# Another order for the first four units of a clustering-and-convolution kernel, with identity products ahead of them

## The chip, the cores and the metric

One core of a Trainium2 chip runs the kernel. The metric is device time in microseconds for one launch, the median of three runs; lower is better.

## The reference

The input `x` is 8 images of 512 channels and 32 x 48 = 1536 pixels, in float32. There are 40 centroids of 512 channels, a 512 x 512 weight matrix and a bias.

```python
xn = x / norm(x, axis=1); cn = centroids / norm(centroids, axis=1)
sim = einsum('bchw,nc->bnhw', xn, cn)
idx = argmax(sim, axis=1)
onehot = one_hot(idx, N)
sum_x = einsum('bhwn,bchw->bnc', onehot, x)
centroids_local = sum_x / maximum(sum(onehot, axis=(1, 2)), 1.0)[..., None]
gathered = centroids_local[arange(B)[:, None, None], idx]
delta = transpose(gathered, (0, 3, 1, 2)) - x
alpha = exp(-mean(delta * delta, axis=1, keepdims=True))
y = x + alpha * delta
out = relu(einsum('oc,bchw->bohw', W, y) + b)
```

So each pixel finds its nearest centroid by cosine, each image makes its own means of the pixels of a cluster, each pixel is pulled towards its cluster's mean, and a 1 x 1 convolution with bias and relu follows.

## The kernel before

The work is cut into 24 units of 512 pixels, three to an image; unit g belongs to image g // 3. Channels lie on partitions in four blocks of 128. Each engine has a list of instructions of its own, written out by hand in the order in which it runs them, and semaphores tie the lists together. Nothing is reordered: an instruction that waits holds back all behind it on its engine.

Image b's first half is the clustering. `similarities(g)` on TensorE makes products of 64 x 256 with the centroids as weights (L696). `copy_sims` on ScalarE keeps the result (L546). `transpose_sims` brings the similarities of the image into pixels by centroids (L705). `argmax` is five VectorE operations (L320 to L332) that give `oh`, the one-hot. `copy_onehot` makes bfloat16 copies of it (ScalarE, L551), `transpose_onehot` transposes it (TensorE, L720), `evacuate_onehot` copies it out and counts it (ScalarE, L558), and `counts` on VectorE turns the counts into reciprocals (L338, L340). `sum_clusters(b, u)` (TensorE, L737) sums the pixels of a cluster; for that it needs x with pixels on partitions, in `XT`. ScalarE keeps the high half of the sums (`copy_sums`, L564), VectorE the rest (`low_clusters`, L345), TensorE adds the two column halves (`add_halves`, L748 and L749), ScalarE scales them (`means`, L569 and L572), and VectorE splits them into three bfloat16 parts (L351, L354) and writes them to `G` (L359).

Its second half goes unit by unit: `gather(g, h)` (TensorE, L768) multiplies G by the one-hot; `delta` (VectorE, L366) subtracts x; `square` (ScalarE, L513) and `add_squares` (VectorE, L372 to L376), `high_sum` (L518), `low_sum` (L381) and `sum_squares` (TensorE, L775 and L776; L782 for units 0 and 1, in float32) give the mean square; `exp` (L522), `scale` (L386) and `y_half` (GpSimd L281, for unit 0 VectorE L394) give y; `high_half` (ScalarE, L527) and `low_half` (GpSimd, L288) split y into two parts; `convolve` (L794 to L796) makes three products for each pair of blocks, and `relu` (L535) writes the output tile. The convolution runs two units behind the gather.

How `XT` is filled differs. For image 0 TensorE transposes x in blocks (`transpose_x(u, half)`, L806: half 0 into `main`, half 1 into `gat`), and VectorE (`keep_transposed(u)`, L303, half 0 of units 0 and 1) or ScalarE (L502, the others) copies the result out of PSUM. From image 1 on x is loaded a second time in blocks of 32 channels (`load_xs`, L210, four transfers of 256 KB per unit), and VectorE transposes these in 32 x 32 squares (`transpose_half(g, h)`, L311); the second one signals `tr_done`, on which `load_xs(g + 4)` and later waits.

The loads are all issued on SyncE's queue, in the order of its list: centroids, x of units 0 to 2, the weights, the bias, x of units 3 and 4, the blocks of unit 3, x of unit 5, the blocks of unit 4, and so on. x loads are L204. The weights `W` are transposed on TensorE (`transpose_weights`, L820) once the copies of x have left `main` and `gat`.

The order on TensorE at the start is written at L830 to L849: similarities 0, both halves of unit 0's transposes, similarities 1 and 2, and so on. ScalarE's stands at L590 to L630.

```python
            similarities(0)
            transpose_x(0, 0)
            transpose_x(0, 1)
            similarities(1)
            similarities(2)
            transpose_x(1, 0)
            transpose_sims(0)
            transpose_x(1, 1)
```

Of the kernel before, what the change touches and what calls it, by code (L numbers as in the profile page):

```python
# [14 lines left out]
P = 128  # L15
# [3 lines left out]
PARTS = HW // UNIT  # L19
# [43 lines left out]
def build(nc, x, cent, w, bias, out):  # L63
# [3 lines left out]
    with ctx:  # L67
# [130 lines left out]
        def _(sp):  # L198
# [24 lines left out]
            with nc.allow_non_contiguous_dma(reason="512 bias values, once"):  # L223
                sp.dma_start(bcol[:, :], bias.rearrange("(k p) -> p k", p=P)).then_inc(b_in, 16)
            load_x(3)
            load_x(4)
            load_xs(3)
            load_x(5)
# [69 lines left out]
        def _(dve):  # L298
            v_ = nc.vector

            def keep_transposed(u):
                dve.wait_ge(xp_done, 2 * u + 1)
                v_.tensor_copy(XT[:, u, 0:HALF, :], main[:, :, :]).then_inc(xe_dve, 1)  # L303

# [121 lines left out]
            dve.wait_ge(const_done, 7)  # L426
            keep_transposed(0)
            keep_transposed(1)
            argmax(0)
            for k in range(KC):  # L430
                low_weights(k)
            low_clusters(0)
            counts(0)
            transpose_half(3, 0)
            rest_of_mean(0)
            parts_of_mean(0)

            transpose_half(3, 1)
            for g in range(DIRECT):
# [57 lines left out]
        def _(act):  # L497
# [91 lines left out]

            copy_sims(0)  # L590
            keep_transposed(0, 1)
            copy_sims(1)
            copy_sims(2)
            keep_transposed(1, 1)
            keep_transposed(2, 0)
# [24 lines left out]
            relu(0, 1)  # L620
            high_half(1, 1)
            square(2, 0)
            copy_sums(1)
            square(2, 1)
            evacuate_onehot(1)
            means(1)
            high_sum(2)
            relu(0, 2)
# [48 lines left out]
        def _(pe):  # L677
# [45 lines left out]
            def sum_clusters(b, u):  # L723
                if u == 0:
                    pe.wait_ge(oh_done, b + 1)
                    wait(pe, sumsL_done, b)
                if b > 0:
                    pe.wait_ge(tr_done, PARTS * (b - 1) + u + 1)
                elif u < PARTS - 1:
                    pe.wait_ge(xe_dve, u + 1)  # L730
                    pe.wait_ge(xe_act, u + 1)
                else:
                    pe.wait_ge(xe_act, PARTS + 1)
                for t in range(HALF):
                    for h in range(2):
                        tile = HALF * h + t
                        last = t_.matmul(sumP[NPAD * h:NPAD * (h + 1), :], oh[:, slot(u, tile), :],  # L737
                                         XT[:, u, tile, :], start=(u == 0 and t == 0),
                                         stop=(u == PARTS - 1 and t == HALF - 1))
                last.then_inc(c_done, 1)  # L740
# [60 lines left out]
            def transpose_x(u, half):  # L801
                wait(pe, (xe_dve, xe_act)[half], u)
                for t in range(HALF):
# [4 lines left out]
                last.then_inc(xp_done, 1)  # L808

            pe.wait_ge(ident_done, 5)  # L810
            pe.wait_ge(c_in[0], 16)
            for k in range(KC):
                last = t_.transpose(sumP[:, k * N:(k + 1) * N], craw[0:N, k * P:(k + 1) * P], ident[0:N, 0:N])
            last.then_inc(cT_ps, 1)
            pe.wait_ge(cT_done, 2)
            def transpose_weights(k):
                pe.wait_ge(w_in, 16)
                pe.wait_ge(xe_act, 3 if k < 2 else 4)
                for o in range(KC):
# [10 lines left out]
            similarities(0)  # L830
            transpose_x(0, 0)
            transpose_x(0, 1)
            similarities(1)
            similarities(2)
# [99 lines left out]
```

## Time and profile before

| what | value |
|---|---|
| median of 3 runs | 435.92 us (435.83 to 436.05) |
| the profiled execution's own time | 435.22 us |
| its span, first to last instruction | 433.4 us |
| TensorE busy | 420.2 us (97%), 2112 instructions |
| VectorE busy | 286.6 us (66%) |
| ScalarE busy | 242.4 us (56%) |
| GpSimd busy | 206.5 us (48%) |
| chain that ended last | TensorE 92%, GpSimd 2%, ScalarE 2% |
| DMA | 73.94 MB, mean 171 GB/s |

The span is what the profile's rows cover; 1.8 us of the profiled time lie around it. The chain is followed back from the last instruction, at each step to what released it. A busy share is an average over the span; the stages at the start differ from the rest, and for them the timeline is read. In the rows, PE is TensorE, DVE VectorE, ACT ScalarE, POOL GpSimd and SP SyncE. A float32 product stands in the timeline as two passes, a 128 x 128 transpose as one.

### The profile page before, as it was taken

What the parts mean: (1) busy time and instruction counts of PE and PEld (TensorE: products, weight loads), DVE (VectorE), ACT (ScalarE), POOL (GpSimd) and SP (SyncE); (2) the same over time, 40 slices, a digit from 0 to 9 for tenths busy, and PEclk for the clock granted to TensorE, in tenths of its full rate; (3) what the DMA queues carried; (4) which work ended last, traced back from release to release, by engine and by line L of the source; (5) the groups of instructions that cost most, each with busy time, mean ns of one, the idle gap of its engine ahead of it and who ended that gap; (6) DMA issues with size and microseconds to landing.
All of it is one profiled execution on the core that took longest, in us unless ns stands there. A gap on an engine that the chain in (4) does not pass through costs nothing.

```text
span 433.4 us, 5744 instructions
## 1 busy us (share of the span) xinstructions
PE 420.2 (97%) x2112; PEld 292.9 (68%) x2112; DVE 286.6 (66%) x378; ACT 242.4 (56%) x328; POOL 206.5 (48%) x102
## 2 busy tenths in 40 slices
PE   4999989999999999999999999999999999999997
PEld 2745446775777767775767757776677758777785
DVE  2549959495684767586773956857674956777730
ACT  5465374565563674554754665646735647555542
POOL 2000572585373681764644852835816645334330
PEclk9999999999999999999999999999999999999999
DMA  8996296977489755859279664888564220222133
GB/s 285 343 228 131 49 255 174 280 226 181 133 210 241 190 198 112 240 143 284 97 195 228 196 161 147 228 208 200 189 140 151 99 97 2 98 98 97 42 113 136
DMA packets 70927, 73.94 MB, mean 171 GB/s; under 512 B 2724, under 2 KB 45732, under 8 KB 70900
## 3 DMA queue, kind: packets, MB, share of 16 engines
q1 hardware_dynamic: 70900, 73.58, 61.4%
q8 instruction: 17, 0.28, 0.3%
q14 instruction: 10, 0.08, 0.1%
HBM read 48.40 MB, written 25.17 MB: 170 GB/s over the span
## 4 chain that ended last, share of the span: by engine, by line
PE 92%; POOL 2%; ACT 2%; DMA 1%; DVE 1%; issue 1%; SPq 0%
PE main L794 20%; PE main L796 20%; PE main L795 20%; PE fa L696 10%; PE sump L737 9%; PE gat L768 5%; PE al L775 1%; DMA x<-x 1%; POOL yl L288 1%; PE fa L705 1%; PE al L776 1%; PE fa L720 1%; POOL z L281 1%; PE gat L782 1%; PE al L782 1%; ACT oht L558 1%
## 5 line engine op out<-in xcount | busy, mean ns | idle before, releaser
L281 POOL TENSOR_TENSOR z<-z,x 128x1024 f32<-128x1024 f32 x42 | 99.3, 2383 | 154.3 <-DVE z L386 154.3
L794 PE MATMUL main<-yh,wh 128*128 128x512 f32 x376 | 153.1, 407 | 0.0
L796 PE MATMUL main<-yh,wl 128*128 128x512 f32 x376 | 147.2, 391 | 0.0
L795 PE MATMUL main<-yl,wh 128*128 128x512 f32 x376 | 147.0, 391 | 0.0
L288 POOL TENSOR_TENSOR yl<-z,yh 128x1024 fp32r<-128x1024 f32 x44 | 105.8, 2420 | 54.9 <-ACT yh L527 54.9
L366 DVE TENSOR_TENSOR z<-gat,x 128x1024 f32<-128x1024 f32 x46 | 56.1, 1220 | 91.4 <-PE gat L768 91.3
L535 ACT ACTIVATE o<-main,bcol 128x512 f32<-128x512 f32 x96 | 65.8, 687 | 85.4 <-PE main L796 85.4
L794 PEld LDWEIGHTS main<-yh,wh 128*128 128x128 f32 x376 | 70.6, 188 | 20.8 <-issue 4.6
L796 PEld LDWEIGHTS main<-yh,wl 128*128 128x128 f32 x376 | 70.6, 188 | 15.8
L795 PEld LDWEIGHTS main<-yl,wh 128*128 128x128 f32 x376 | 70.8, 188 | 14.5
L527 ACT ACTIVATE yh<-z 128x1024 fp32r<-128x1024 f32 x48 | 50.5, 1052 | 22.9 <-POOL z L281 21.9
L386 DVE TENSOR_TENSOR z<-z,al 128x1024 f32<-128x1024 f32 x46 | 53.9, 1211 | 1.5 <-ACT al L522 1.5
L311 DVE STREAM_TRANSPOSE xt<-xs 128x1024 f32<-128x1024 f32 x42 | 51.0, 1228 | 0.0
L696 PE MATMUL fa<-x,c_t 128*64 128x256 f32 x384 | 46.7, 394 | 3.5 <-DMA x<-x 3.2
L737 PE MATMUL sump<-xt,oh 128*64 128x512 f32 x192 | 43.6, 598 | 0.0
L696 PEld LDWEIGHTS fa<-x,c_t 128*64 128x64 f32 x384 | 27.4, 140 | 21.4 <-issue 10.7
L513 ACT ACTIVATE sq<-z 128x1024 f32<-128x1024 f32 x22 | 23.3, 1060 | 21.9 <-DVE z L366 21.9
L513 ACT ACTIVATE gat<-z 128x1024 f32<-128x1024 f32 x22 | 22.6, 1027 | 18.8 <-DVE z L366 18.8
L737 PEld LDWEIGHTS sump<-xt,oh 128*64 128x64 f32 x192 | 12.9, 136 | 25.5 <-issue 25.5
L768 PE MATMUL gat<-oht,g 120*128 120x512 bf16 x92 | 27.9, 385 | 0.4 <-DVE g L359 0.2
L518 ACT ACTIVATE sh<-al 128x512 fp32r<-128x512 f32 x22 | 13.2, 598 | 8.7 <-DVE al L376 8.7
L522 ACT ACTIVATE al<-al 128x512 f32<-128x512 f32 x23 | 13.6, 590 | 7.8 <-PE al L776 6.5
(111 smaller groups left out, 316.6 us busy)
## 6 DMA issues: line engine op xcount, KB each, us to landing
x<-x SPq DMA_DIRECT2D x24, 1024.0 KB, 5.5
out<-o SPq DMA_DIRECT2D x23, 1024.0 KB, 4.7
xs<-x SPq DMA_DIRECT2D x84, 256.0 KB, 5.8
o<-w SPq DMA_DIRECT2D x1, 1024.0 KB, 11.9
out<-o SPq DMA_DIRECT2D x4, 256.0 KB, 2.1
sq<-centroids SPq DMA_DIRECT2D x2, 80.0 KB
bcol<-bias SPq DMA_DIRECT2D x1, 2.0 KB, 11.5
```

Source lines behind the costliest of these rows:

```text
L281: pool.tensor_tensor(z, z, X[g // PARTS % 2][:, pair(h), span(g)], ALU.add).then_inc(y_pool, 1)
L288: pool.tensor_tensor(YL[g % 2][:, pair(h), :], Z[g % 2][:, pair(h), :], YH[g % 2][:, pair(h), :].bitcast(F32), ALU.subtract).then_inc(lo_p ...
L311: last = v_.transpose(XT[:, g % PARTS, :, :].rearrange("p t (m j) -> p m t j", j=BLK)[:, blocks, :, :], XS[g % 2][:, blocks, :])
L366: v_.tensor_tensor(Z[g % 2][:, pair(h), :], banks(g, h)[:, :, :], X[g // PARTS % 2][:, pair(h), span(g)], ALU.subtract).then_inc(z_done, 1)
L386: v_.tensor_tensor(z, z, alpha(g).unsqueeze(1).to_broadcast([P, 2, UNIT]), ALU.mult).then_inc(za_done, 1)
L527: a_.activation(YH[g % 2][:, pair(h), :], Z[g % 2][:, pair(h), :], ACT.Copy).then_inc(hi_done, 1)
L535: a_.activation(OUT[g % 2][:, o, :], main[:, o % 2, :], ACT.Relu, bias=bcol[:, o:o + 1]).then_inc(relu_done, 1)
L696: last = t_.matmul(simP[u][NPAD * h:NPAD * (h + 1), :], cT[:, k, :], toks, start=(k == 0), stop=(k == KC - 1))
L737: last = t_.matmul(sumP[NPAD * h:NPAD * (h + 1), :], oh[:, slot(u, tile), :], XT[:, u, tile, :], start=(u == 0 and t == 0), stop=(u == PAR ...
L794: t_.matmul(main[:, o % 2, :], WH[:, k, rows], YH[g % 2][:, k, :], start=(k == 0), stop=False)
L795: t_.matmul(main[:, o % 2, :], WH[:, k, rows], YL[g % 2][:, k, :], start=False, stop=False)
L796: last = t_.matmul(main[:, o % 2, :], WL[:, k, rows], YH[g % 2][:, k, :], start=False, stop=(k == KC - 1))
```

## The change

Five things are done, all in the first four units.

- TensorE multiplies the identity by itself into `al`, twice ahead of the centroids' transposes and nine times behind them (`keep_busy`). The result is not used.
- TensorE's order: similarities 1 now stands ahead of the second half of unit 0's transposes, so similarities 2 comes behind it. ScalarE's copies follow this.
- Half 0 of unit 1's transposed x is copied out by ScalarE and no longer by VectorE; the waits on `xe_dve` and `xe_act` are renumbered.
- VectorE's two transposes of unit 3's blocks stand ahead of the low half of the cluster sums and ahead of the counts; before, one stood behind the counts and one behind G. SyncE issues the blocks of unit 3 ahead of x of unit 4.
- ScalarE, in image 1: the one-hot's evacuation stands ahead of the upper squares of unit 2, and the upper high half of unit 1 behind the means.

```diff
             load_x(3)
+            load_xs(3)
             load_x(4)
-            load_xs(3)
             load_x(5)
...
-            keep_transposed(0)
-            keep_transposed(1)
+            keep_transposed()
             argmax(0)
             for k in range(KC):
                 low_weights(k)
+            transpose_half(3, 0)
             low_clusters(0)
+            transpose_half(3, 1)
             counts(0)
-            transpose_half(3, 0)
             rest_of_mean(0)
             parts_of_mean(0)
 
-            transpose_half(3, 1)
...
             copy_sims(0)
+            copy_sims(1)
             keep_transposed(0, 1)
-            copy_sims(1)
             copy_sims(2)
+            keep_transposed(1, 0)
             keep_transposed(1, 1)
...
-            high_half(1, 1)
             square(2, 0)
             copy_sums(1)
+            evacuate_onehot(1)
             square(2, 1)
-            evacuate_onehot(1)
             means(1)
+            high_half(1, 1)
             high_sum(2)
...
+            def keep_busy(times):
+
+                for _ in range(times):
+                    t_.matmul(al[:, 0:P], ident[:, :], ident[:, :], start=True, stop=True)
+
             pe.wait_ge(ident_done, 5)
+            keep_busy(2)
             pe.wait_ge(c_in[0], 16)
...
             last.then_inc(cT_ps, 1)
+            keep_busy(9)
             pe.wait_ge(cT_done, 2)
...
             similarities(0)
             transpose_x(0, 0)
+            similarities(1)
             transpose_x(0, 1)
-            similarities(1)
             similarities(2)
```

TensorE from its first instruction to the first weights' transposes, before (`sump` holds the centroids' transposes, `fa` the similarities, `main` and `gat` the transposed x):

```order
L813 MATMUL sump<-ident,sq 128x40 x4
L696 MATMUL fa<-x,c_t 64x256 x8
L806 MATMUL main<-ident,x 128x128 x8
L806 MATMUL gat<-ident,x 128x128 x8
L696 MATMUL fa<-x,c_t 64x256 x16
L806 MATMUL main<-ident,x 128x128 x8
L705 MATMUL fa<-ident,sims 128x128 x6
L806 MATMUL gat<-ident,x 128x128 x8
L806 MATMUL main<-ident,x 128x128 x8
L806 MATMUL gat<-ident,x 128x128 x8
L820 MATMUL main<-ident,o 128x128 x8
```

and with the change, whose line numbers differ by a few:

```order
L815 MATMUL al<-ident 128x128 x2
L821 MATMUL sump<-ident,sq 128x40 x4
L815 MATMUL al<-ident 128x128 x9
L696 MATMUL fa<-x,c_t 64x256 x8
L808 MATMUL main<-ident,x 128x128 x8
L696 MATMUL fa<-x,c_t 64x256 x8
L808 MATMUL gat<-ident,x 128x128 x8
L696 MATMUL fa<-x,c_t 64x256 x8
L808 MATMUL main<-ident,x 128x128 x8
L705 MATMUL fa<-ident,sims 128x128 x6
L808 MATMUL gat<-ident,x 128x128 x8
L808 MATMUL main<-ident,x 128x128 x8
```

The identity products stand around the centroids' transposes, and the first 24 similarities and 16 transposes alternate in groups of eight; from the transposes of unit 1 on the order is the old one.

VectorE behind the low halves of the weights, to unit 0's first delta (L311 transposes unit 3's blocks, L345 is the low half of the sums, L338 and L340 are the counts, L351 to L359 make G), one piece of the difference:

```order
-L345 TENSOR_TENSOR sums_l<-sump,sums_h 128x512
-L338 TENSOR_SCALAR cols<-cols 120x1
-L340 RECIPROCAL cols<-cols 120x1
-L311 STREAM_TRANSPOSE xt<-xs 128x8x4x32
+L311 STREAM_TRANSPOSE xt<-xs 128x8x4x32
+L345 TENSOR_TENSOR sums_l<-sump,sums_h 128x512
+L311 STREAM_TRANSPOSE xt<-xs 128x8x4x32
+L338 TENSOR_SCALAR cols<-cols 120x1
+L340 RECIPROCAL cols<-cols 120x1
 L351 SCALAR_TENSOR_TENSOR al<-part,cols,al 120x512
 L354 CAST part<-al 120x512
 L359 SCALAR_TENSOR_TENSOR g<-part,cols,al 120x512
-L311 STREAM_TRANSPOSE xt<-xs 128x8x4x32
 L366 TENSOR_TENSOR z<-gat,x 128x1024
```

Both transposes moved: the first from behind the counts to ahead of the low half, the second from behind G to ahead of the counts.

ScalarE in image 1, from the first relu of unit 0 to the means (L513 squares, L564 the sums, L558 the one-hot's evacuation, L569 and L572 the means, L527 a high half), before:

```order
L535 ACTIVATE o<-main,bcol 128x512 x2
L527 ACTIVATE yh<-z 128x1024
L513 ACTIVATE sq<-z 128x1024
L564 ACTIVATE sums_h<-sump 128x512
L513 ACTIVATE gat<-z 128x1024
L558 ACTIVATE oht,cols<-fa 120x1536
L569 ACTIVATE fa<-fa,cols 120x512
L572 ACTIVATE part<-fa 120x512
L518 ACTIVATE sh<-al 128x512
```

and with the change:

```order
L534 ACTIVATE o<-main,bcol 128x512 x2
L512 ACTIVATE sq<-z 128x1024
L563 ACTIVATE sums_h<-sump 128x512
L557 ACTIVATE oht,cols<-fa 120x1536
L512 ACTIVATE gat<-z 128x1024
L568 ACTIVATE fa<-fa,cols 120x512
L571 ACTIVATE part<-fa 120x512
L526 ACTIVATE yh<-z 128x1024
L517 ACTIVATE sh<-al 128x512
```

The upper high half of unit 1 moved from the second row to the last but one, and the evacuation moved past one square.

## Rows read from the trace of the kernel before

**Rows 1.** Windows, all engines: stretch, length, busy us (count), clock, DMA, GB/s.
```profile
100.00:200.00 100.00, 100.00 (x507) 70.31 (x506) 69.27 (x82) 57.69 (x78) 56.76 (x24) 1.00 0.69 188
```

**Rows 2.** Timeline, PE, 0 to 35 us: start, us, engine, line, what [idle before].
```profile
2.84 0.62 PE L813 MATMUL sump<-ident,sq 40*128 40x40 f32 x4 [2.84 <-DMA sq<-centroids]
...
6.68 3.68 PE L696 MATMUL fa<-x,c_t 128*64 128x256 f32 x16 [3.23 <-DMA x<-x]
...
12.26 3.67 PE L696 MATMUL fa<-x,c_t 128*64 128x256 f32 x32
...
21.66 1.94 PE L737 MATMUL sump<-xt,oh 128*64 128x512 f32 x8
...
34.65 0.60 PE L768 MATMUL gat<-oht,g 120*128 120x512 bf16 x2 [0.24 <-DVE g L359]
```

**Rows 3.** Timeline: PE's float32 products of 512 columns, GpSimd's identity.
```profile
39.23 3.60 PE L782 MATMUL al<-o,ones 128*128 128x512 f32 x8
...
42.66 3.60 PE L782 MATMUL gat<-o,ones 128*128 128x512 f32 x8
...
1.52 0.29 POOL L261 TENSOR_SCALAR_AFFINE_SELECT ident<-ident 128x128 f32<-128x128 f32 x1 [0.24 <-POOL cols L259]
```

**Rows 4.** SP issues at 2.1, 18.0, 19.4, landings, all x loads' landings, one window.
```profile
2.13 0.93 SPq L204 DMA_DIRECT2D x<-x  x2
...
DMA to landing us min/median/max: 7.4/8.5/9.6
...
18.02 1.30 SPq L210 DMA_DIRECT2D xs<-x  x1
...
xs<-x SPq DMA_DIRECT2D x1, 256.0 KB, 10.1
...
19.36 3.12 SPq L204 DMA_DIRECT2D x<-x  x1
...
DMA to landing us min/median/max: 5.3/9.6/14.6
...
17.00:18.00 1.00, 1.00 (x12) 1.00 (x11) 1.00 (x1) 0.00 (x0) 0.00 (x0) 1.00 1.05 397
```

**Rows 5.** Timeline, DVE and ACT, 18 to 36 us.
```profile
18.13 0.65 DVE L320 TENSOR_REDUCE best<-fa 128x12 f32<-128x480 f32 x1
...
29.05 1.45 ACT L558 ACTIVATE oht<-fa 120x1536 bf16<-120x1536 bf16 x1 [0.20 <-PE fa L720]
...
30.62 0.15 DVE L338 TENSOR_SCALAR cols<-cols 120x1 f32<-120x1 f32 x1 [1.05 <-ACT oht L558]
...
30.89 1.25 DVE L311 STREAM_TRANSPOSE xt<-xs 128x1024 f32<-128x1024 f32 x1
...
33.85 0.75 DVE L359 SCALAR_TENSOR_TENSOR g<-part,cols,al 120x512 bf16<-120x512 bf16 x1
...
35.67 1.19 DVE L366 TENSOR_TENSOR z<-gat,x 128x1024 f32<-128x1024 f32 x1
```

**Rows 6.** Timeline, ACT, PE, DVE and POOL, 57 to 69 us.
```profile
57.96 1.06 ACT L527 ACTIVATE yh<-z 128x1024 fp32r<-128x1024 f32 x1
...
60.35 1.02 ACT L513 ACTIVATE gat<-z 128x1024 f32<-128x1024 f32 x1
...
61.30 1.44 ACT L558 ACTIVATE oht<-fa 120x1536 bf16<-120x1536 bf16 x1
...
62.88 0.49 PE L748 MATMUL fa<-sums_h,select 128*120 128x512 f32 x1 [1.99 <-ACT oht L558]
...
63.12 0.67 DVE L372 TENSOR_TENSOR sq<-sq,gat 128x512 f32<-128x512 f32 x1
...
67.31 0.74 DVE L359 SCALAR_TENSOR_TENSOR g<-part,cols,fa 120x512 bf16<-120x512 bf16 x1
...
68.36 0.59 PE L794 MATMUL main<-yh,wh 128*128 128x512 f32 x1
...
57.89 4.69 POOL L288 TENSOR_TENSOR yl<-z,yh 128x1024 fp32r<-128x1024 f32 x2
```

More of the change, by code:

```diff
@@ L299, in _, with keep_transposed @@
             v_ = nc.vector
-            def keep_transposed(u):
-                dve.wait_ge(xp_done, 2 * u + 1)
-                v_.tensor_copy(XT[:, u, 0:HALF, :], main[:, :, :]).then_inc(xe_dve, 1)
+            def keep_transposed():
+                dve.wait_ge(xp_done, 1)
+                v_.tensor_copy(XT[:, 0, 0:HALF, :], main[:, :, :]).then_inc(xe_dve, 1)
             def transpose_half(g, h):
@@ L728, in sum_clusters @@
                     pe.wait_ge(tr_done, PARTS * (b - 1) + u + 1)
-                elif u < PARTS - 1:
-                    pe.wait_ge(xe_dve, u + 1)
-                    pe.wait_ge(xe_act, u + 1)
-                else:
-                    pe.wait_ge(xe_act, PARTS + 1)
+                else:
+                    pe.wait_ge(xe_dve, 1)
+                    pe.wait_ge(xe_act, 2 * u + 1)
                 for t in range(HALF):
@@ L801, in transpose_x @@
             def transpose_x(u, half):
-                wait(pe, (xe_dve, xe_act)[half], u)
+                if (u, half) == (1, 0):
+                    pe.wait_ge(xe_dve, 1)
+                elif u > 0:
+                    pe.wait_ge(xe_act, 2 * (u - 1) + half)
                 for t in range(HALF):
@@ L817, in transpose_weights @@
                 pe.wait_ge(w_in, 16)
-                pe.wait_ge(xe_act, 3 if k < 2 else 4)
+                pe.wait_ge(xe_act, 4 if k < 2 else 5)
                 for o in range(KC):
```

## The prediction

> **What bounds the kernel now.** I read three views in order. First the windows: from 100 to 200 us TensorE is busy for all of the 100 us [rows 1], and the shares of the page say the same of the whole (97%). So the steady part is a fixed amount of TensorE work, and a change to the first 70 us can only move it as a block, by the idle or slow TensorE time that it removes there. Second, TensorE's own timeline, to find such time [rows 2]. There are three stretches. (a) The first similarities take 3.68 us for 16 passes, from 6.68; the next row has 32 of the same passes in 3.67 us. TensorE had done 0.62 us of work, at 2.84, and was idle until x landed. The granted clock column shows 1.00 in all windows, but the durations show the lower level (1.2 GHz) in the first and the higher (2.4 GHz) in the second; everything after 10.30 runs at the higher. (b) From 29.05 [rows 5] to 34.65 [rows 2] the mean of image 0 is made on ScalarE and VectorE, with little TensorE work beside it. (c) Before 62.88 TensorE is idle for 1.99 us, waiting for ScalarE's one-hot evacuation [rows 6]. Third, what ends these: the loads [rows 4], the mean chain [rows 5] and ScalarE's order in image 1 [rows 6].
>
> **Step 1, products with the identity.** 2 + 9 products, 128 columns each, in float32. The trace has none. The nearest row is the 512-column float32 product: 8 passes, four products, start to start 3.43 us (39.23 to 42.66), so 0.86 us each and by columns 0.215 us for 128 at the high level, 0.43 at the low one [rows 3]. The identity is ready at 1.52 + 0.29 = 1.81 [rows 3], so two products run 1.9 to 2.8, just before the centroid transposes at 2.84, which end at 3.46; a delay of 0.1 us there is covered, because the similarities wait for x until 6.68 [rows 2]. The other nine take 3.9 us at the low level and end at 7.3; if the level rises as long after the start of work as it did in this trace (6.68 to 10.30, 3.6 us, so at about 5.5), five of them are slow, four are fast, and they end near 6.5. I estimate an overrun over 6.68 of 0.2 us (bounds 0 and 0.6). The first similarities then take 1.84 instead of 3.68: a gain of 1.84 less 0.2. Bounds: 1.84, and, if nothing rises in time, a loss of 0.6.
>
> **Step 2, unit 2's similarities earlier, copies moved.** The same TensorE work as before stands from there to 21.66, in another order, so only new waits count. Similarities 0 end at 8.5 to 8.7, the eight transposes at 9.6 (0.97 us: sixteen of them stand between 10.30 and 12.26). Unit 1's x was issued at 2.13 and takes 7.4 us: 9.5, and the start about 0.13 later, as at 6.68; unit 2's takes 9.6 from about 2.6: 12.2 [rows 4]. The walk then reads: similarities 1 until 11.5, transposes 12.5, similarities 2 until 14.3, half 0 of unit 1's transposes 15.2, the transposed similarities 15.9. So there are waits of 0.1 to 0.2 us for x, in total 0.2. VectorE loses one copy to ScalarE and starts the argmax at 16.0 instead of 18.13; its five operations, of 0.65 us like the first [rows 5], take 3.4 us with their gaps, so the one-hot is there at 19.4. ScalarE now has four copies of 1.03 us in a row, from 15.3 to 20.2, each released by a block of transposes of the same length; as before, TensorE waits some 0.2 us for one of them, a wait that exists already. The cluster sums of unit 0 start at 20.1 instead of 21.66 [rows 2]. What remains of step 1 and 2: 1.84 - 0.2 - 0.2, **1.4 us**.
>
> **Step 3, VectorE's transposes and the load order.** Each of unit 3's two transposes takes 1.25 us. They stood in the mean chain: one at 30.89, beside ScalarE's means, and one behind G, which kept delta at 35.67 although G was done at 33.85 + 0.75 = 34.60 [rows 5]. Now the first stands ahead of the low half of the cluster sums, the second between it and the counts. The chain's times shift by 1.4: ScalarE keeps the sums at 26.9 and gives the one-hot at 30.60 - 1.4 = 29.2 (evacuation 29.05 plus 1.45 and the count [rows 5]). The first transpose fits if unit 3's blocks have landed by 26.1; the second runs 28.1 to 29.3 beside the evacuation, so the counts start 0.1 late at most. The blocks: the last was issued at 18.02 and took 10.1 us, 28.1 [rows 4]. The change puts them ahead of unit 4's x, 1.05 MB at 397 GB/s, so 2.6 us earlier [rows 4]: 25.5. It fits by 0.6 us. Unit 4's x falls back to where the blocks were, 28.1 at most; its similarities come at 31.1. Unit 5's, issued at 19.36, lands by 34.0 even with the longest time seen, 14.6 [rows 4], and its similarities start at 34.2. Delta gains 0.4 us more than TensorE, but TensorE has similarities 5 in between and did not wait for delta, so I cost that at nothing. The first gather moves from 34.65 to 33.25: the 1.4 us are kept. From there to 58 us everything is the old order, shifted; GpSimd's chain begins with unit 0's high half, which shifts too.
>
> **Step 4, ScalarE in image 1.** Before: high half (1,1) at 57.96, square (2,0), sums, square (2,1) at 60.35, evacuation 61.30 to 62.83, TensorE on at 62.88 [rows 6]. Now (in the times of before) square (2,0) starts at 57.8, the sums at 58.7, the evacuation when TensorE's one-hot transposes end, 59.45, and it is done at 61.0. TensorE reaches the sum of halves at 60.9: its wait of 1.99 goes to 0.1, **1.85 us gained** there. What is late next: square (2,1) runs 60.9 to 61.9 (before it ended at 61.37), and VectorE's in-order row behind it starts at 61.95 instead of 63.12: squares, rest of the mean, low sum, G, in all 4.93 us (63.12 to 67.31 + 0.74 [rows 6]), so G is there at about 66.7 against 68.05. TensorE, 1.85 early, would reach unit 3's gather at 66.3 and waits 0.4 for it. What remains is **1.4 us** (bounds: 0, if the chain behind square (2,1) does not move, and 1.85). High half (1,1) goes from 57.96 to about 63.4 to 64.4, behind the means; GpSimd then needs 2.35 us for its low half (4.69 for two), 66.8. TensorE wants it in the middle of the convolution that started at 68.36, seven products in, now at 68.5: covered, by 1.7 us [rows 6].
>
> **The sum.** 1.4 + 1.4 = 2.8 us. The profiled execution took 435.22, so it would be 432.4; the median of the runs shown, 435.92, is 0.7 above it, and against that I forecast **433.1**. A measurement can tell about 0.2%, 0.9 us, from no change.
>
> **Rivals.** *The clock does not rise in time* (chance 0.15). The products may be too few, or too loosely spaced around 2.8 us, so that the similarities start at 7.3 and still take 3.68: steps 1 and 2 lose 0.6 instead of gaining 1.4, the whole gains 0.8, 435.1. For it: the only rise in the trace came after 3.6 us of dense work. Against it: the products offer 4.8 us of nearly dense work before x lands. The Trainium skill (TensorE: Matmul & The Clock Gate, Part 1) says that the point of the rise differs from run to run of the same kernel. By that the executions would scatter by up to 1.8 us of lost or gained clock; the three runs lie within 0.22 us of each other, so the runs here speak against it, and that is why this rival gets no more.
>
> *Only step 1 to 3 pays* (0.12). ScalarE's new order moves the wait from 62.88 to unit 3's gather, with the sum of squares and G later than worked out: the whole gains 1.4, 434.5. For it: G was done at 68.05, and the convolution behind unit 3's gather started at 68.36, so G already bounds together with TensorE.
>
> *Unit 3's blocks land late* (0.10, of it 0.04 slower). VectorE is in order, and the first transpose now stands ahead of the sums' low half, the counts, the mean and G. The point from which it costs is a landing at 26.1; after that each us late is a us. At 28.1, the old landing, the counts start at 28.1 + 1.25 + 0.65 + 1.25 = 31.25 instead of 30.62: steps 1 to 3 lose 0.6, the whole gains 0.8, 435.1. From 28.9 on the kernel is **slower**: with the last block issued at 18.02 and the longest time of any x load, 14.6, it would be 32.6, 3.7 us over the old time, 439.6; in the middle, at 30.7, 437.7. Against it: the same bytes with one megabyte less ahead.
>
> **How the numbers follow.** The forecast has 0.60 and its own bounds (overrun 0 to 0.6, G's 0 to 0.4) give 432.3 to 433.8; the three rivals 0.37; 0.03 is left for more than I count. The range 432.2 to 435.0 takes the forecast, the second rival and the cases between it and the first. Faster by over 0.2%: 0.60 + 0.12 + 0.03 and most of the cases between forecast and first and third rival, 0.87; within 0.2%: 0.09; slower: 0.04.
>
> **What would show it.** Right: the similarities of unit 0 have 16 passes in about 1.8 us and start at 6.7 to 6.9; the one-hot is done by 19.5; unit 3's first transpose starts by 26.1 with no wait behind it; the first gather is at about 33.2; the wait before the sum of halves of image 1 is under 0.3 us and unit 3's gather comes 2.8 us earlier, at 65.3. Wrong: passes of 630 ns at 6.7 us, VectorE idle before the first transpose beyond 26.1, or a new TensorE wait at the low half (1,1).

## The result and the profile after

| | before | with the change |
|---|---|---|
| median of 6 runs each | 435.99 us (435.75 to 436.52) | 433.12 us (432.35 to 433.72) |
| ratio, 95% interval | | 0.9931 [0.9918, 0.9944] |
| the profiled execution | 435.22 us, span 433.4 | 433.72 us, span 431.9 |
| TensorE busy | 420.2 us (97%) | 424.5 us (98%) |
| TensorE's share of the chain | 92% | 95% |

The ratios here and below are of the means. One execution of the kernel before, among those run beside e5 to e8, took 533.62 us at a mean granted clock of 0.757 and is in no comparison.

The median fell by 2.87 us where 2.8 were forecast. But the two profiled executions are only 1.5 us apart, so a profile read against a profile shows half of the gain, and the first question is where the other half is. The table already gives part of the answer: the profiled execution of before is faster than all six timed ones, and that of the change is the slowest of its six.

The window of the steady part is what it was [rows 1]:

```profile
100.00:200.00 100.00, 100.00 (x508) 70.39 (x506) 68.59 (x83) 57.92 (x78) 56.79 (x24) 1.00 0.70 188
```

TensorE's timeline of the change answers to [rows 2] (start, us, engine, line, what):

```profile
1.87 1.23 PE L815 MATMUL al<-ident 128*128 128x128 f32 x4 [1.87 <-POOL ident L261]
3.03 0.65 PE L821 MATMUL sump<-ident,sq 40*128 40x40 f32 x4
3.61 4.21 PE L815 MATMUL al<-ident 128*128 128x128 f32 x18
7.74 2.43 PE L696 MATMUL fa<-x,c_t 128*64 128x256 f32 x16
10.11 1.09 PE L808 MATMUL main<-ident,x 128*128 128x128 f32 x8
...
21.64 1.94 PE L736 MATMUL sump<-xt,oh 128*64 128x512 f32 x8
...
34.64 0.60 PE L767 MATMUL gat<-oht,g 120*128 120x512 bf16 x2 [0.24 <-DVE g L359]
```

The two first products take 1.16 us up to the centroids' transposes, which are 0.2 late, and the nine take 4.13 us, 0.46 each: all at the lower level (421 ns is the median of a pass, against 274 to 275 ns in the faster part of e6 below). The similarities begin at 7.74, 1.06 later than in the trace of before, and are themselves slow for a while: 2.37 us up to 10.11, where 1.88 is the time at the higher level. The clock rose at about 8.8 (if t us were slow, t/3.62 + (2.37 - t)/1.88 = 1, so t = 1.0), not at 5.5. The cluster sums start at 21.64 against 21.66: in this execution steps 1 and 2 of the prediction gave nothing.

VectorE, 17 to 36 us, against [rows 5]:

```profile
17.69 0.66 DVE L320 TENSOR_REDUCE best<-fa 128x12 f32<-128x480 f32 x1 [5.16 <-PE fa L705]
...
26.04 1.23 DVE L311 STREAM_TRANSPOSE xt<-xs 128x1024 f32<-128x1024 f32 x1
...
29.47 1.23 DVE L311 STREAM_TRANSPOSE xt<-xs 128x1024 f32<-128x1024 f32 x1
30.63 0.13 DVE L338 TENSOR_SCALAR cols<-cols 120x1 f32<-120x1 f32 x1
...
33.83 0.75 DVE L359 SCALAR_TENSOR_TENSOR g<-part,cols,al 120x512 bf16<-120x512 bf16 x1
35.28 1.23 DVE L366 TENSOR_TENSOR z<-gat,x 128x1024 f32<-128x1024 f32 x1 [0.70 <-PE gat L767]
```

The first transpose starts as soon as VectorE is free, with no wait for its blocks. The second ends just as the counts can start. Delta now starts 0.39 us earlier than it did.

Image 1, against [rows 6], in the order PE, ACT, DVE, POOL:

```profile
45.98 1.94 PE L736 MATMUL sump<-xt,oh 128*64 128x512 f32 x8
60.95 0.49 PE L747 MATMUL fa<-sums_h,select 128*120 128x512 f32 x1 [0.18 <-ACT oht L557]
65.99 0.47 PE L774 MATMUL al<-sh,ones 128*128 128x512 f32 x1 [0.22 <-DVE sl L381]
66.56 0.60 PE L767 MATMUL gat<-oht,g 120*128 120x512 bf16 x2
66.81 0.59 PE L793 MATMUL main<-yh,wh 128*128 128x512 f32 x1
...
59.35 1.45 ACT L557 ACTIVATE oht<-fa 120x1536 bf16<-120x1536 bf16 x1
60.79 1.02 ACT L512 ACTIVATE gat<-z 128x1024 f32<-128x1024 f32 x1
63.25 1.05 ACT L526 ACTIVATE yh<-z 128x1024 fp32r<-128x1024 f32 x1
...
61.84 0.69 DVE L372 TENSOR_TENSOR sq<-sq,gat 128x512 f32<-128x512 f32 x1 [0.57 <-ACT gat L512]
65.77 0.73 DVE L359 SCALAR_TENSOR_TENSOR g<-part,cols,fa 120x512 bf16<-120x512 bf16 x1
...
64.38 2.39 POOL L288 TENSOR_TENSOR yl<-z,yh 128x1024 fp32r<-128x1024 f32 x1 [4.13 <-ACT yh L526]
```

This is step 4 as it was read: TensorE's wait of 1.99 is 0.18, the new bound is the low sum and G behind the upper squares (a wait of 0.22 at 65.99), and GpSimd's low half, 64.38 to 66.8, ends before it is wanted. From the first cluster sums of image 1 to unit 3's gather it was 68.11 - 46.19 = 21.92 us and is 66.56 - 45.98 = 20.58: 1.34 gained, forecast 1.4.

Four of the signs that the prediction named for being right fail in this execution: the similarities of unit 0 start at 7.74 and not by 6.9, the argmax starts only at 17.69 (its five operations end at 21.1, not by 19.5), the first gather is at 34.64 and not near 33.2, and unit 3's gather at 66.56 and not at 65.3. A better execution comes close (e4, below: similarities at 6.91, gathers at 33.32 and 65.22).

### The profile page after: what moved, and what is told of

Read it like the earlier page. It is cut to its first block, busy times and chain, and to the rows that moved or that the text cites. A ratio compares the mean times of both kernels' runs of the same rounds, so it can differ in the third digit from the quotient of the medians.

```text
span 431.9 us, 5788 instructions
## 1 busy us (share of the span) xinstructions
PE 424.5 (98%) x2134; PEld 296.9 (69%) x2134; DVE 285.3 (66%) x377; ACT 243.7 (56%) x329; POOL 206.8 (48%) x102
## 4 chain that ended last, share of the span: by engine, by line
PE 95%; DVE 2%; ACT 1%; issue 1%; POOL 0%; POOLq 0%; DVEq 0%
PE main L793 20%; PE main L795 19%; PE main L794 19%; PE sump L736 10%; PE fa L696 9%; PE gat L767 5%; PE al L774 1%; PE al L815 1%; PE fa L705 1%; PE al L775 1%; PE fa L720 1%; PE main L836 1%; PE al L781 1%; PE gat L781 1%; DVE xt L311 1%; PE gat L808 1%
## 5 line engine op out<-in xcount | busy, mean ns | idle before, releaser
L311 DVE STREAM_TRANSPOSE xt<-xs 128x1024 f32<-128x1024 f32 x42 | 51.0, 1228 | 0.0
L696 PE MATMUL fa<-x,c_t 128*64 128x256 f32 x384 | 45.7, 386 | 0.3 <-ACT oht L557 0.3
L736 PEld LDWEIGHTS sump<-xt,oh 128*64 128x64 f32 x192 | 12.8, 136 | 25.5 <-issue 25.5
## 6 DMA issues: line engine op xcount, KB each, us to landing
o<-w SPq DMA_DIRECT2D x1, 1024.0 KB, 12.2
bcol<-bias SPq DMA_DIRECT2D x1, 2.0 KB, 11.7
```

What stands on the lines that cost most here:

```text
L311: last = v_.transpose(XT[:, g % PARTS, :, :].rearrange("p t (m j) -> p m t j", j=BLK)[:, blocks, :, :], XS[g % 2][:, blocks, :])
L696: last = t_.matmul(simP[u][NPAD * h:NPAD * (h + 1), :], cT[:, k, :], toks, start=(k == 0), stop=(k == KC - 1))
```

## Experiments

The runs came in three sets, e1 to e4, e5 to e8 and e9 to e12, each on a chip of its own, with the kernel before run beside each set. Its median was 435.91, 435.85 and 435.56 us, so between sets a difference of 0.3 us says little. My theory after reading both traces: ScalarE's order gives its 1.4 to 1.5 us in every execution, and the products give the rest through the clock, by an amount that differs from execution to execution. Rivals: the new order of similarities, copies and loads gives the rest; or the products cost what they give.

### The parts alone

`e1_no_products`, the change without its products:

```diff
-            keep_busy(2)
...
-            keep_busy(9)
```

> The change without its eleven identity products. Theory (the clock is worth 1.3 us in the median, ScalarE's order in image 1 the rest, 1.55): 434.4 against 436.0 before, and in the profile the first similarities start at 6.7 and need about 3.6 us. Rival (the new order of similarities, copies and loads brings the 1.3 us, the products nothing): 433.1. Rival 2 (the products cost as much as they give): 433.1 or less as well.

`e2_products_only`, before with the products:

```diff
+            keep_busy(2)
             pe.wait_ge(c_in[0], 16)
...
+            keep_busy(9)
             pe.wait_ge(cT_done, 2)
```

> The kernel before with the eleven products and nothing else. Theory: 434.7, with a larger scatter between the executions than the kernel before, because the point at which the clock rises moves from run to run; the first similarities start between 6.7 and 7.8 and take 1.8 to 3.7 us. Rival (order): 436.0.

`e3_act_order_only`, before with ScalarE's order:

```diff
-            high_half(1, 1)
             square(2, 0)
             copy_sums(1)
+            evacuate_onehot(1)
             square(2, 1)
-            evacuate_onehot(1)
             means(1)
+            high_half(1, 1)
```

> The kernel before with only ScalarE's new order in image 1. Theory: 1.55 us less than before, 434.4; TensorE's wait before the sum of halves of image 1 falls from 1.99 to under 0.3 us and unit 3's first convolution starts 1.5 us earlier. Rival (the wait only moves to unit 3's gather): 435.5 or more.

`e4_seven`, the change with seven products in place of nine:

```diff
-            keep_busy(9)
+            keep_busy(7)
```

> The change with 7 instead of 9 products behind the centroids' transposes. Theory (nine overrun x's landing by up to 1.0 us when all of them run at the low level, 4.21 us for nine): 432.8, up to 0.5 us less than the change where the clock rises late, the same where it rises early. Rival (the last two products are what brings the rise ahead of the similarities): 433.5 or more.

| run | median us (lowest to highest), executions | ratio to before [95%] |
|---|---|---|
| e1, no products | 433.81 (433.61 to 434.19), 5 | 0.9955 [0.9942, 0.9968] |
| e2, products only | 434.63 (433.85 to 436.22), 12 | 0.9978 [0.9965, 0.9991] |
| e3, ScalarE's order only | 434.07 (433.89 to 434.72), 5 | 0.9964 [0.9952, 0.9975] |
| e4, seven products | 433.15 (432.40 to 433.33), 5 | 0.9936 [0.9924, 0.9949] |

The kernel before stood at 435.91 there (435.02 to 436.49, 17 executions). ScalarE's order alone takes 1.84 off the median, the products alone 1.28, and without the products the change loses 0.7. So the rival that gave the rest to the new orders falls with e1, though by less than forecast (433.81, not 434.4). The parts add up to more than the whole (1.84 + 1.28 against 2.87): with five executions in a run, a median carries some tenths of a us of scatter. In the trace of e3 the wait before the sum of halves is 0.18:

```profile
61.94 0.49 PE L748 MATMUL fa<-sums_h,select 128*120 128x512 f32 x1 [0.18 <-ACT oht L558]
```

Both e3 and e1 have the first similarities at the lower level throughout; e1's rows:

```profile
6.66 3.68 PE L696 MATMUL fa<-x,c_t 128*64 128x256 f32 x16 [3.09 <-DMA x<-x]
10.27 1.22 PE L808 MATMUL main<-ident,x 128*128 128x128 f32 x8
```

With seven products the median is that of nine; the expected 432.8 was not reached. Its profiled execution (432.40) shows what a good one looks like: similarities at the high level from their first pass, waiting for x where in the change x waited for them, and the cluster sums at 20.32.

```profile
3.60 3.15 PE L815 MATMUL al<-ident 128*128 128x128 f32 x14
6.91 1.95 PE L696 MATMUL fa<-x,c_t 128*64 128x256 f32 x16 [0.16 <-DMA x<-x]
...
20.32 1.94 PE L736 MATMUL sump<-xt,oh 128*64 128x512 f32 x8
```

What was not expected stands in e2. Its 12 executions are two groups: seven from 433.85 to 435.00 with a mean granted clock of 1.000, and five from 435.61 to 436.22 with 0.996. The profiled one (435.61) is of the second group. Its windows (stretch, length, busy PE, PEld, DVE, ACT, POOL, clock, DMA, GB/s) and its PE rows in image 1:

```profile
60.00:62.00 2.00, 0.01 (x1) 0.01 (x1) 0.32 (x2) 1.94 (x3) 1.70 (x1) 0.99 1.22 206
62.00:63.00 1.00, 1.00 (x3) 0.79 (x3) 0.96 (x4) 0.00 (x0) 0.00 (x0) 0.50 1.22 217
...
65.00:66.00 1.00, 1.00 (x5) 0.77 (x5) 0.97 (x2) 0.69 (x2) 0.00 (x0) 0.81 1.04 383
```

```profile
61.99 0.78 PE L748 MATMUL fa<-sums_h,select 128*120 128x512 f32 x1 [2.01 <-ACT oht L558]
62.57 0.63 PE L749 MATMUL fa<-sums_l,select 128*120 128x512 f32 x1
...
65.72 0.40 PE L795 MATMUL main<-yl,wh 128*128 128x512 f32 x1
```

The granted clock falls to 0.50, the lower level, at the end of the 2.01 us in which TensorE waits for ScalarE's evacuation, and comes back at about 65.4 (0.81 is the mean of the window from 65 to 66). Meanwhile products start 0.43 us apart instead of 0.23, and 1.5 us are lost: from the first cluster sums of image 1 to the gather it is 68.73 - 45.28 = 23.45 us instead of 21.92. Half the clock for 3.4 us takes 0.4% off the mean over the span, which is what a mean of 0.996 says. The kernel before has the same wait, 1.99 us in its profiled execution, and a mean clock of 1.000 in all 17 executions.

### Undoing one step each, and moving the products

`e5_old_act`, the change with ScalarE's order put back (the diff of e3, reversed).

> The change with ScalarE's order in image 1 put back to the old one. Theory (with the products the clock falls to the lower level in some executions, when TensorE idles 2.0 us before the sum of halves of image 1, as in the run with the products alone): two groups of executions, one near 434.0 with a granted clock of 1.000 and one 1.7 us above it with 0.996; median between 434.0 and 435.7. Rival (that fall belonged to the old order of similarities or loads): one group near 434.7, clock 1.000 in all.

`e6_products_act`, before with the diffs of e2 and e3 and nothing else.

> The kernel before with the products and ScalarE's new order in image 1, without the new orders of similarities, copies, transposes and loads. Theory (those orders bring 0.3 us or less): 433.0 to 433.4, granted clock 1.000 in every execution. Rival (the new orders are worth 1 us, since x's similarities follow its landing): 434.0 or more.

`e7_old_loads`, the change with the old order of loads:

```diff
             load_x(3)
-            load_xs(3)
             load_x(4)
+            load_xs(3)
```

> The change, but unit 3's blocks are issued behind unit 4's x, as before. Theory (VectorE runs in order, and a landing later than 26.1 holds back the counts and G): the first transpose starts at about 28.1, the counts at about 31.2, the first gather at 35.2 or 35.3 whatever the clock did, so 434.4, with a smaller scatter than the change. Rival (the transposes' place makes no difference): 433.1.

`e8_early`, the change with the products on a tile of their own:

```diff
+            v_.memset(hot[:, :], 1.0).then_inc(hot_done, 1)
             v_.memset(cT[:, :, N:NPAD], 0.0).then_inc(cT_done, 1)
...
-                    t_.matmul(al[:, 0:P], ident[:, :], ident[:, :], start=True, stop=True)
+                    t_.matmul(al[:, 0:P], hot[:, :], hot[:, :], start=True, stop=True)
...
+            pe.wait_ge(hot_done, 1)
+            keep_busy(4)
             pe.wait_ge(ident_done, 5)
-            keep_busy(2)
...
-            keep_busy(9)
+            keep_busy(7)
```

> The change with the products on a tile that VectorE fills as its first operation: four ahead of the centroids' transposes, from 1.0 us instead of 1.87, and seven behind them. Theory (the earlier dense work starts, the earlier the clock rises in the unlucky executions): 432.8, and the slowest execution 433.3 or less. Rival (the point of the rise does not follow the start of the work that closely): 433.1, scatter as in the run with seven.

| run | median us (lowest to highest), executions | ratio to before [95%] |
|---|---|---|
| e5, change with ScalarE's old order | 434.26 (433.71 to 436.40), 12 | 0.9980 [0.9965, 0.9995] |
| e6, products and ScalarE's order | 432.90 (432.30 to 433.10), 5 | 0.9928 [0.9916, 0.9940] |
| e7, change with the old loads | 435.61 (433.85 to 438.20), 12 | 1.0002 [0.9981, 1.0023] |
| e8, products early | 432.58 (432.29 to 432.65), 5 | 0.9923 [0.9911, 0.9935] |

The kernel before stood at 435.85 there (434.90 to 436.53, 22 executions).

e5 falls into the two groups that the theory named: seven executions from 433.71 to 434.30 with a clock of 1.000, five from 435.94 to 436.40 with 0.996. Its profiled execution is of the first group: TensorE waits 2.11 us before the sum of halves and the clock does not fall. So such a wait does not bring the fall each time, and where the clock fell in the other five is not shown.

e6 is as fast as the change (a little below the 433.0 to 433.4 expected), so steps 2 and 3, the orders of similarities, copies, transposes and loads, bring nothing together that these runs can tell. The intervals of the timelines say why. From the transposes behind the first similarities to the cluster sums it is 11.45 us in e6, with a short wait for x in it (11.30 in e2 and in e10), and 11.53 in the change (10.11 to 21.64); from there to image 1's first cluster sums 24.52 in e6 and 24.34 in the change.

```profile
3.60 3.22 PE L813 MATMUL al<-ident 128*128 128x128 f32 x18
6.75 1.95 PE L696 MATMUL fa<-x,c_t 128*64 128x256 f32 x16
8.63 1.09 PE L806 MATMUL main<-ident,x 128*128 128x128 f32 x8
...
20.08 1.94 PE L737 MATMUL sump<-xt,oh 128*64 128x512 f32 x8
...
44.60 1.94 PE L737 MATMUL sump<-xt,oh 128*64 128x512 f32 x8
```

Eight passes of similarities and eight transposes in turn cost 0.2 more (11.53 against 11.30, both without a wait for x), the earlier delta gives 0.2 back. The products of e6, up to 5.5 us and from 5.65 on (ns, shortest, median, longest of a pass), show where its clock rose:

```profile
L813 PE MATMUL al<-ident x9: 348/421/580, 3.6 to 5.5; 128*128 128x128 f32 x9
...
L813 PE MATMUL al<-ident x11: 274/275/421, 5.3 to 6.5; 128*128 128x128 f32 x11
```

In e7 the blocks land at 28.06, and VectorE stands still for them (the last figure is its idle time):

```profile
28.06 1.25 DVE L311 STREAM_TRANSPOSE xt<-xs 128x1024 f32<-128x1024 f32 x1 [2.19 <-DMA xs<-x]
...
30.95 0.11 DVE L338 TENSOR_SCALAR cols<-cols 120x1 f32<-120x1 f32 x1
```

```profile
29.00:30.00 1.00, 0.00 (x0) 0.00 (x1) 1.00 (x3) 1.00 (x1) 0.00 (x0) 1.00 1.24 204
```

The counts start at 30.95 and the first gather at 34.94, where 31.2 and 35.2 were expected. But this is a good execution (433.96): the three with a clock of 0.999 lie between 433.85 and 434.03, six with 0.996 from 435.02 to 436.07 and three with 0.992 at 438.1. The window from 29 to 30 has no TensorE work at all. The mean clocks of the other nine are those of one fall like e2's (0.996) and of two (0.992), and the median loses 2.5 us on the change instead of the 1.3 I had worked out. So the price of late blocks is not the us of the wait alone. Where the clock fell in these nine is not shown, since none of them was profiled; the longest wait of TensorE in the profiled one is only 1.28 us (28.75 to 30.03). The scatter was expected smaller than the change's and came larger.

e8 is the fastest of its set: 0.54 us under the change's median in the first table (0.57 under e4's and 0.7 under e11's, all of other sets), and its slowest execution, 432.65, is faster than five of the change's six. Seven products behind the transposes brought nothing by themselves (e4), so the gain is that of the earlier start and the two more products ahead; that the tile holds ones and not the identity was not tried apart. TensorE starts 0.82 us sooner:

```profile
1.05 2.07 PE L818 MATMUL al<-hot 128*128 128x128 f32 x8 [1.05 <-DVE hot L410]
...
3.63 2.85 PE L818 MATMUL al<-hot 128*128 128x128 f32 x14
6.66 1.95 PE L699 MATMUL fa<-x,c_t 128*64 128x256 f32 x16 [0.19 <-DMA x<-x]
...
20.23 1.94 PE L739 MATMUL sump<-xt,oh 128*64 128x512 f32 x8
```

### The wait filled, the change again, half of step 4

`e9_early_act`, before with ScalarE's order (the diff of e3) and the early products (the diff of e8).

> The kernel before with two things: the early products (a tile of their own from 1.0 us, four and seven) and ScalarE's new order in image 1. Theory (the other orders bring nothing): 432.4 to 432.7, as the change with early products; granted clock 0.999 or 1.000 in every execution. Rival (with the clock early, the order of similarities begins to pay): 433.0 or more.

`e10_filled_wait`, before with the products (the diff of e2) and seven more in the wait:

```diff
             convolve(0, 2, range(0, 2))
+            pe.wait_ge(sumsL_done, 2)
+            for _ in range(7):
+                t_.matmul(sumP[:, 0:P], ident[:, :], ident[:, :], start=True, stop=True)
             add_halves(1)
```

> The kernel before with the eleven products at the start, ScalarE's order as before, and seven more identity products inside TensorE's 2.0 us wait in image 1, behind the wait for the sums' low half. Theory (TensorE's idleness in that wait is what lets the clock fall in some executions): no execution with 0.996, one group, median 434.0 to 434.4, against two groups and 434.63 without the filling. Rival (the fall comes from elsewhere): still two groups, some executions near 436.0 at 0.996.

`e11_change_again` is the change itself.

> The change itself once more, for its scatter and a second profile. Theory (the point of the rise moves from execution to execution): median 433.0 to 433.2, from 432.3 to 433.7; the first similarities start between 6.7 and 7.8 and the first cluster sums between 20.1 and 21.7, together with the execution's time. Rival (the first profile shows the usual case, and the median's gain is from something else): the first similarities again start at 7.7 and the first cluster sums at 21.6, whatever the time.

`e12_high_back`, the change with this:

```diff
+            high_half(1, 1)
             square(2, 0)
             copy_sums(1)
             evacuate_onehot(1)
             square(2, 1)
             means(1)
-            high_half(1, 1)
```

> The change, with the upper high half of unit 1 put back ahead of the lower squares of unit 2; the evacuation stays ahead of the upper squares. Theory (the high half's 0.95 us stand ahead of the evacuation and of the upper squares, and all behind them up to G follow): TensorE waits 0.9 to 1.0 us before the sum of halves, unit 3's gather comes 0.85 later, 433.9 to 434.0. Rival (the evacuation ahead of the squares is all that matters, the high half fits beside): 433.1 to 433.3.

| run | median us (lowest to highest), executions | ratio to before [95%] |
|---|---|---|
| e9, early products and ScalarE's order | 432.59 (432.24 to 433.56), 6 | 0.9932 [0.9920, 0.9943] |
| e10, products, wait filled | 434.56 (433.69 to 435.09), 8 | 0.9974 [0.9964, 0.9984] |
| e11, the change again | 433.29 (432.62 to 433.35), 5 | 0.9939 [0.9926, 0.9952] |
| e12, high half back | 434.02 (433.36 to 434.45), 5 | 0.9959 [0.9948, 0.9971] |

The kernel before stood at 435.56 there (435.08 to 436.34, 13 executions).

e10: with products in the wait no execution shows 0.996; all eight are at 0.999 or 1.000, in one group. This supports that the idleness of TensorE there is what the fall needs. The fall had come in 10 of the 24 executions of e2 and e5. At that share eight in a row without one come by chance about once in 75 times, and e10 ran on another chip than they, so this is strong but no proof. The runs with the products and ScalarE's new order say the same: apart from e7, which has a wait of its own, the 37 executions of the change, e4, e6, e8, e9, e11 and e12 (which has part of that order) have none under 0.999. The median was expected at 434.0 to 434.4 and came at 434.56. In the profiled execution (433.69) the interval to unit 3's gather is the old one, 66.55 - 44.59 = 21.96 us, so the filling costs nothing there; the scatter of the first rise could make the rest, which is not shown.

```profile
59.65 1.83 PE L888 MATMUL sump<-ident 128*128 128x128 f32 x14 [0.33 <-DVE sums_l L345]
```

e11's profiled execution (433.35) had its similarities from 7.73 to 9.67, 1.94 us, and the cluster sums at 21.21, and lies 0.37 us below the first one (433.72, sums at 21.64). The start at 7.7 is what its rival expected; the level during the similarities is what differs, and the cluster sums came 0.4 us earlier, against the rival.

```profile
7.73 2.01 PE L696 MATMUL fa<-x,c_t 128*64 128x256 f32 x16
21.21 1.94 PE L736 MATMUL sump<-xt,oh 128*64 128x512 f32 x8
```

e12 puts a price on the second half of step 4: TensorE waits 1.14 us, unit 3's gather comes 66.90 - 45.35 = 21.55 us behind image 1's first cluster sums instead of 20.58, and the median is 434.02, as expected. So of the 1.34 us, the evacuation's place gives 0.4 and the high half's place 1.0.

```profile
61.28 0.50 PE L747 MATMUL fa<-sums_h,select 128*120 128x512 f32 x1 [1.14 <-ACT oht L557]
```

e9 equals e8 to within what sets can be compared (432.59 and 432.58; 3.0 and 3.3 us under the kernel before of its own set), and it is 0.7 us faster than e11 beside it: the whole gain of the change, and more, is to be had with the early products and ScalarE's order alone. The early start does not fix the point of the rise: by the spacing of passes it is at 5.8 in e8's profile and at 4.8 in e9's, and e9's executions spread over 1.3 us where e8's spread over 0.4.

One sum ties all profiles together. The time of each profiled execution less the start of its first cluster sums is 412.0 to 412.1 us in e1, e4, e8, e11 and the change, 412.2 to 412.3 in e3, e6 and e9, which lack step 3, and 413.6 in the kernel before and e10, which lack steps 3 and 4. So behind the cluster sums the executions of one kernel hardly differ, step 4 is worth 1.3 us and step 3 0.2, and nearly all of the scatter lies ahead of the cluster sums. With this the medians of the first table stand for cluster sums at about 22.4 us before and 21.0 with the change: 1.4 us for steps 1 and 2, of which the two profiles (21.66 and 21.64) show nothing. That is the other half of the gain.

## Why the prediction was right, and where its steps were not

The time, 433.1, and the sign were right, and the two terms that made it are the two that the runs show: 1.4 us ahead of the cluster sums through the clock, 1.4 us in image 1 through ScalarE's order (measured: about 1.4 in the medians, and 1.3). The second was worked out for the right reason. The first is right as a sum of medians, but part of that is luck: the clock rose later than the prediction had it on both sides. Step by step:

*What bounds the kernel.* Stretch (b) was read wrongly: from 29.05 to 34.65 TensorE is not nearly idle. It has the similarities of units 3 and 4 there (3.67 us from 30.74) and stands still for 0.70, 0.32 and 0.24 us only. No term rests on it.

*Step 1, the products.* The mechanism holds, the times did not. "They end near 6.5" took the rise to come at about 5.5; in the nine profiled executions with the first products at 1.87 the spacing of passes (0.21 us apart at the lower level, 0.11 at the higher) puts it at 5.6 (e6, e10), 6.4 (e4), 7.4 (e2, e5, e12), 7.9 (e11), 8.3 (e7) and 8.8 (the change's first). Nine products that run low take 4.13 us and the similarities start at 7.74, an overrun of 1.06 where I had bounds of 0 and 0.6. The cluster sums start between 20.06 and 21.64 in these. On the side of before I took one execution for all: it had the rise at 10.5 (e1's at 10.6, e3's at 11.7), and was itself the fastest of its kernel until then. The median's gain is this shift of both: 1.17 us between e3 and e6, 0.7 between e1 and e4, and about 1.4 between before and the change, where 1.4 was the term.

*The first rival* said that the executions would scatter, after the Trainium skill (TensorE: Matmul & The Clock Gate, Part 1), and that three runs within 0.22 us speak against it. The page was right and I was wrong to let three runs decide: 17 executions of before spread over 1.5 us, six of the change over 1.4. The profiled execution of the change is this rival in part, the gain of steps 1 and 2 being 0.0 in it.

*Step 2* was costed at 0.2 of waiting. There is no wait in the change's first trace, since the similarities are late themselves; in e8, where they are early, the second group waits for x: it starts at 9.72, 0.16 behind the transposes' usual 1.02 us. The order as such costs 0.2 us.

*Step 3* was costed at nothing, with TensorE not waiting for delta. It gives 0.2 us: image 1's first cluster sums come 24.34 us behind image 0's instead of 24.53. The landing was forecast at 25.5 and came by 26.04 without a wait; e5's transpose starts at 25.41 without one. The third rival's mechanism is real: put in, it costs 2.5 us in the median. "After that each us late is a us" was the failing sentence, since it left the clock out: the good execution of e7 loses only 0.5 us behind its cluster sums (433.96 - 21.39 = 412.57 us, against 412.1), and the rest comes with the lower mean clock of the others.

*Step 4* was right in mechanism and size: G moved from 67.31 to 65.77, of which 1.33 us are gained behind the first cluster sums of image 1, forecast 1.4; the remaining wait, 0.2 where 0.4 was forecast, stands at the sum of squares, and the low half is covered. The sum in it has a slip: 61.95 + 4.93 is 66.88 and not 66.7, which would have given 1.2 and not 1.4. VectorE's row from the squares to the end of G took 4.66 us (61.84 to 65.77 + 0.73) in place of 4.93, and that made up for it. What I did not see is that with products at the start the wait that was removed is also one at which the clock can fall. e5 loses 1.14 us on the change in the median, which is the wait (its group at 1.000 has a median 1.04 above the change's), and its five executions at 0.996 lie another 2.0 above that, the slowest 3.3 above the change.

Steps 2 and 3 together are worth about nothing (e6 against the change, 432.90 and 433.12). The prediction had them at a cost of 0.2, the wait of step 2, and did not say that half of the change could be left out.

## What to carry to other kernels

A saving from the clock's first rise is a distribution, so take it from medians of many executions and not from two profiles, whose difference here was half of the true one. Once TensorE's work at the start is made early, look at the later waits of TensorE, those of 2 us first: removing the one here was worth as much as the products (1.3 us, and in some executions 2 us more), and e7 shows that a change of order can bring falls of the clock with waits that look shorter. Put such filling work on the tile that is ready first: in these runs that gave 0.5 to 0.7 us more.

## What the runs showed of the hardware that I had not expected

- In e2's profiled execution the granted clock fell to 0.50 after TensorE had been idle for 2.01 us, for 3.4 us (62.0 to 65.4), and this cost 1.5 us. The mean clock that goes with such a fall, 0.996, stands in 5 of 12 executions of e2 and 5 of 12 of e5. It stands in none of the 17 executions of the kernel before that ran beside e2, nor in the 35 compared beside the later kernels, though that kernel has the same wait (1.99 us). Why the kernel before is spared stays open.
- The clock of 1.00 that the windows show in the first 10 us is not what the durations show. The passes of the kernel before, from 6.6 to 10.2 us and from 12.2 to 16 us (ns, shortest, median, longest):

```profile
L696 PE MATMUL fa<-x,c_t x16: 630/634/689, 6.7 to 9.7; 128*64 128x256 f32 x16
...
L696 PE MATMUL fa<-x,c_t x32: 378/379/430, 12.3 to 15.6; 128*64 128x256 f32 x32
```

- Transposes keep the higher level. In the change TensorE does transposes alone from 15.91 to 21.64, 46 of them, and the last eight take no longer than the first. In e3, where transposes ran before the rise, they start 0.21 us apart instead of 0.11, so their time does show the level:

```profile
15.91 1.09 PE L808 MATMUL main<-ident,x 128*128 128x128 f32 x8
...
20.65 1.06 PE L829 MATMUL main<-ident,o 128*128 128x128 f32 x8
```

The Trainium skill (TensorE: Matmul & The Clock Gate, Part 4) says that the high level is not engaged for transposes; as to keeping that level, the trace does not agree. Whether transposes alone would raise the clock was not tried.
